# The last phase in sixteen half groups: a ring of seven PSUM banks, root arithmetic in PSUM, and TensorE filled ahead

## The reference

```python
    x = x + _layernorm(_L0_attn_ref(_layernorm(x, axis=-1), ...), axis=-1)
    x = x + _layernorm(_L0_ffn_ref(_layernorm(x, axis=-1), ...), axis=-1)

def _layernorm(x, axis=-1, eps=1e-05):
    m = jnp.mean(x, axis=axis, keepdims=True)
    v = jnp.var(x, axis=axis, keepdims=True)
    return (x - m) / jnp.sqrt(v + eps)
...
        yk = out[slot].reshape(T, K, H)
        y = jnp.sum(yk * topk_w[..., None].astype(yk.dtype), axis=1)
        shared = jax.nn.silu(x @ Sg.T) * (x @ Su.T) @ Sd.T
        return (y + shared).reshape(B, S, H)
```

## Time and profile before

| | |
|---|---|
| median of 3 runs | 1362.87 us (1362.18 to 1364.79) |
| the profiled execution | 1371.37 us |
| its span, first to last instruction | 1369.6 us |
| busy in the span | PE 89%, POOL 68%, DVE 64%, ACT 60% |
| last phase, first load's issue to the end of the span | 1307.87 to 1369.6: 61.7 us |

### The profile page before, as it was taken

One profiled execution on the slowest core, in us unless ns is written; L12 is line 12 of the kernel. 1 busy time (PEld: TensorE's weight loads), 2 busy tenths in 40 slices (PEclk: granted clock), 3 DMA queues, 4 the chain that ended last, 5 costly groups with the idle time before them and its releaser, 6 DMA issues.

```text
span 1369.6 us, 25270 instructions
## 1 busy us (share of the span) xinstructions
PE 1215.2 (89%) x7836; PEld 850.2 (62%) x7836; DVE 873.8 (64%) x2285; ACT 825.7 (60%) x2128; POOL 925.9 (68%) x1126
## 2 busy tenths in 40 slices
PE   2798989999999999999999998998866998999985
PEld 1455656666666666666666666666633677878864
DVE  5799467587679768758777875766765322232236
ACT  2566668867777776777777677777733322333313
POOL 2897556568878877986887797798754523444553
PEclk9999999999999999999999999999978999999966
DMA  7584786755555354445434444444443569898683
GB/s 229 141 221 108 179 227 154 166 108 116 122 99 117 73 111 97 83 93 101 79 79 86 97 75 85 79 72 88 78 112 118 149 183 232 234 241 197 133 252 123
DMA packets 364678, 182.68 MB, mean 133 GB/s; under 512 B 287440, under 2 KB 343222, under 8 KB 364544
## 3 DMA queue, kind: packets, MB, share of 16 engines
q1 hardware_dynamic: 344960, 166.18, 51.8%
q0 software_dynamic: 16416, 11.70, 4.8%
q10 hardware_dynamic: 3168, 3.15, 0.7%
HBM read 75.32 MB, written 64.69 MB: 102 GB/s over the span
## 4 chain that ended last, share of the span: by engine, by line
PE 38%; DVE 20%; DMA 14%; POOL 12%; issue 8%; ACT 5%; SPq 1%; another core or an unknown queue 1%; ACTq 0%; POOLq 0%; DVEq 0%
DMA PT<-PH 7%; PE bank L1035 7%; DMA Y<-W,wix 6%; PE bank L1050 6%; PE bank L1006 6%; POOL P L937 4%; POOL PH L942 4%; DVE nm L1403 4%; PE bank L1021 4%; PE bank L1067 3%; PE bank L1169 3%; PE bank L1128 2%; PE bank L1112 2%; PE bank L1182 2%; POOL BUF L697 2%
## 5 line engine op out<-in xcount | busy, mean ns | idle before, releaser
L937 POOL TENSOR_SCALAR P<-P,rr 128x256 f32<-128x256 f32 x512 | 249.2, 498 | 140.1 <-DVE rr L1399 131.7
L1265 ACT ACTIVATE P<-bank,nm 128x256 f32<-128x256 f32 x512 | 237.2, 468 | 150.5 <-DVE nm L1403 141.5
L942 POOL TENSOR_TENSOR PH<-P,PH 128x512 f16<-128x512 f32 x256 | 295.8, 1170 | 20.5 <-ACT PH L1274 19.4
L1006 PE MATMUL bank<-RB,W 128*128 128x512 f16 x1076 | 257.2, 381 | 9.0 <-ACT Sx L626 4.3
L697 POOL DMA_INDIRECT BUF<-RT,ix x192 | 198.0, 1031 | 96.5 <-issue 42.0
L1035 PE MATMUL bank<-RB 128*128 128x256 f32 x1024 | 243.9, 381 | 3.8 <-issue 2.2
L1050 PE MATMUL bank<-PT,RB 128*128 128x256 f16 x1536 | 197.7, 274 | 37.7 <-DMA PT<-PH 34.1
L1403 DVE TENSOR_REDUCE nm<-bank 128x2 f32<-128x512 f32 x256 | 174.3, 681 | 52.7 <-PE bank L1035 52.3
L1050 PEld LDWEIGHTS bank<-PT,RB 128*128 128x128 f16 x1536 | 145.8, 98 | 97.1 <-DMA PT<-PH 50.7
L1035 PEld LDWEIGHTS bank<-RB 128*128 128x128 f32 x1024 | 184.6, 190 | 26.9 <-issue 3.9
L1274 ACT ACTIVATE PH<-P 128x512 f16<-128x512 f32 x256 | 161.4, 630 | 57.6 <-POOL P L937 37.1
(11 more groups left out here) (200 smaller groups left out, 1617.7 us busy)
## 6 DMA issues: line engine op xcount, KB each, us to landing
RB<-in_ewT SPq DMA_DIRECT2D x24, 352.0 KB
BUF<-zrow SPq DMA_DIRECT2D x4, 1926.0 KB, 8.4
W<-BUF SPq DMA_DIRECT2D x64, 120.4 KB
HT<-in_ewT SPq DMA_DIRECT2D x18, 352.0 KB
HT<-in_wc SPq DMA_DIRECT2D x24, 256.0 KB, 4.7
HT<-in_ws SPq DMA_DIRECT2D x24, 256.0 KB, 5.0
Y<-zrow SPq DMA_DIRECT2D x10, 512.0 KB, 4.0
RB<-in_ewd SPq DMA_DIRECT2D x24, 176.0 KB
```

The lines of the kernel that those rows point to most:

```text
L937: r = eng.tensor_scalar(p, p, rr[:, w % 4, t:t + 1], SP_, ALU.mult, ALU.mult)
L942: eng.tensor_tensor(PH[:, w % 2, 1, :], P[:, w % 2, :], PH[:, w % 2, 0, :], ALU.subtract).then_inc(s["pl"], 1)
L1006: r = eng.matmul(bk_[:, :], W[:, m, a, c * 2048 + h * 128:c * 2048 + (h + 1) * 128], XT[:, bp % 2, b, c, :], start=(k == 0), stop=(k == n ...
L1265: r = eng.activation(P[:, u % 2, t * 256:(t + 1) * 256], bS[u % 2][:, t * 256:(t + 1) * 256], ACT.Exp, bias=nm0[:, u % 4, t:t + 1], accum_ ...
```

## The change

The unit becomes the half: index i from 0 to 15 is half i % 2 of group `GROUPS[i // 2]`, and the two late groups, 6 and 7, come first. `LB_` is a ring of seven banks with one half each. The eighth, `bP0`, holds mean, variance and the root's working values (`root`, `MV_`) and, in its upper 256 columns, a scratch product. Before the first sum TensorE writes `YL` of halves 0 to 3, then the overflow of halves 0 to 6, then eight times the same product into the scratch. From then on it takes the sum of half i and the overflow of half i + 4, which waits until half i - 3 has left its bank. The inverse root is computed as b = v*y, b = -0.5*b*y, y = (b + 1.5)*y, with v and b in PSUM and y in SBUF. Halves 13 and 15 (`MIXED`) are finished otherwise: ScalarE adds the bias to `x1`, and VectorE makes scale times bank plus that (`last_mixed`). All other residuals are POOL's. POOL's order is written anew.

```diff
-BATCH = ((0, 1), (2, 3), (4, 5), (6,), (7,))
-POOL_LAST = "s0 s1 s2 s3 x0 s4 x1 s5 x2 x3 s6 s7 x4 x5 x6 x7"
+GROUPS = (6, 7, 0, 1, 2, 3, 4, 5)
+BATCH = ((0, 1), (2, 3, 4), (5, 6, 7), (8, 9, 10), (11, 12, 13), (14, 15))
+MIXED = (13, 15)
+AHEAD = 4
+REPEATS = 8
+POOL_LAST = ("s0 s1 s2 s3 s4 s5 s6 s7 x0 s8 x1 s9 x2 s10 x3 s11 x4 s12 x5 s13 x6 s14 x7 s15 "
+             "x8 x9 x10 x11 x12 x14").split()
+DVE_LAST = "b0 b1 b2 b3 b4 b5 v13 v15".split()
...
-        LB_ = ((bACC[0], bACC[1]), (bV, bO), (bS[0], bS[1]), (bP0, bP1))
+        LB_ = (bACC[0], bACC[1], bV, bO, bS[0], bS[1], bP1)
+        NL = len(LB_)
+        root = bP0[:, 0:64].rearrange("p (k t) -> p k t", k=2)
+        MV_ = bP0[:, 128:192].rearrange("p (t n) -> p t n", n=2)
...
+            def last_part(i, part):
+                g, h = place(i)
+                if i >= NL and part != "sum" and (part == "yl" or g < LATE):
+                    if i - NL in MIXED:
+                        eng.wait_ge(s["fy"], MIXED.index(i - NL) + 1)
+                    else:
+                        eng.wait_ge(s["fn"], PLAIN.index(i - NL) + 1)
+                if part == "sum":
+                    eng.wait_ge(s["fa"], i + 1)
...
+            LATER = [i for i in range(2 * NP) if place(i)[0] >= LATE]
+            for i in LATER:
+                last_part(i, "yl")
             for k in range(4):
                 eng.wait_ge(s_o95[k], 16 * E // 4)
...
+            for i in range(NL):
+                last_part(i, "over")
+            for _ in range(REPEATS):
+                eng.matmul(bP0[:, 256:512], ident[:, :], YL[LATE][:, 0, :], start=True, stop=True)
+            for i in range(2 * NP):
+                last_part(i, "sum")
+                if NL <= i + AHEAD < 2 * NP:
+                    last_part(i + AHEAD, "over")
...
-                v, y, a, b = (fNW[:, k, c0:c1] for k in range(4))
-                step(eng.tensor_scalar(v, fMV[:, c0:c1, 1], EPS, None, ALU.add))
+                v, b = (root[:, k, c0:c1] for k in range(2))
+                y, bias = fNW[:, 1, c0:c1], fNW[:, 3, c0:c1]
+                step(eng.tensor_scalar(v, MV_[:, c0:c1, 1], EPS, None, ALU.add))
                 step(eng.tensor_scalar(y.bitcast(I32), v.bitcast(I32), -0.5, RSQRT_MAGIC, ALU.mult, ALU.add))
                 for k in range(3):
-                    step(eng.tensor_tensor(a, y, y, ALU.mult))
-                    step(eng.scalar_tensor_tensor(out=b, in0=a, scalar=-0.5, in1=v, op0=ALU.mult, op1=ALU.mult))
+                    step(eng.tensor_tensor(b, v, y, ALU.mult))
+                    step(eng.scalar_tensor_tensor(out=b, in0=b, scalar=-0.5, in1=y, op0=ALU.mult, op1=ALU.mult))
                     step(eng.scalar_tensor_tensor(out=y, in0=b, scalar=1.5, in1=y, op0=ALU.add, op1=ALU.mult))
...
+            def last_mixed(i):
+                g, h = place(i)
+                eng.wait_ge(s["fb"], MIXED.index(i) + 1)
+                for t in range(2):
+                    c, k = 2 * i + t, 2 * h + t
+                    r = eng.scalar_tensor_tensor(out=fin[g][:, 0, k, :], in0=LB_[i % NL][:, t * 256:(t + 1) * 256],
+                                                 scalar=fNW[:, 1, c:c + 1], in1=x1[g][:, k, :],
+                                                 op0=ALU.mult, op1=ALU.add)
+                r.then_inc(s["fy"], 1)
```

More of the change, by code:

```diff
@@ L29 @@
 SG, SA = 64.0, 64.0
-BATCH = ((0, 1), (2, 3), (4, 5), (6,), (7,))
-POOL_LAST = "s0 s1 s2 s3 x0 s4 x1 s5 x2 x3 s6 s7 x4 x5 x6 x7"
+GROUPS = (6, 7, 0, 1, 2, 3, 4, 5)
+BATCH = ((0, 1), (2, 3, 4), (5, 6, 7), (8, 9, 10), (11, 12, 13), (14, 15))
+MIXED = (13, 15)
+PLAIN = [i for i in range(16) if i not in MIXED]
+AHEAD = 4
[3 more added lines that the diff above has]
+DVE_LAST = "b0 b1 b2 b3 b4 b5 v13 v15".split()
 EPS = 1e-5
@@ L336, in build @@
         names = ("c0 cg cd gt S e r pn ph pl pv oh ol wo q ql k kl v vh vl xc po wm wh wl "
-                 "lf lc xr fo hd bi yi dd lb sw swh swl sg ssl saf sah sal sdn sy et ebt eg esl eac eo eow wix wt wtc fa fp fd fs fn fx fy").split()
+                 "lf lc xr fo hd bi yi dd lb sw swh swl sg ssl saf sah sal sdn sy et ebt eg esl eac eo eow wix wt wtc fa fp fd fs fn fb fx fy").split()
         s = {n: sem(f"s_{n}") for n in names + ["mx"]}
@@ L748, in build, with batch_of, place @@
         plan["sp"].setdefault(END + 101, []).append(last_rows)
-        LB_ = ((bACC[0], bACC[1]), (bV, bO), (bS[0], bS[1]), (bP0, bP1))
+        LB_ = (bACC[0], bACC[1], bV, bO, bS[0], bS[1], bP1)
+        NL = len(LB_)
+        root = bP0[:, 0:64].rearrange("p (k t) -> p k t", k=2)
+        MV_ = bP0[:, 128:192].rearrange("p (t n) -> p t n", n=2)
         def half(a, h):
             return a[:, 2 * h:2 * h + 2, :].rearrange("p t n -> p (t n)")
-        def batch_of(g):
-            return [g in b for b in BATCH].index(True)
+        def batch_of(i):
+            return [i in b for b in BATCH].index(True)
+        def place(i):
+            return GROUPS[i // 2], i % 2
         def run_plan(who, eng, slot, k=0, n=1):
@@ L893, in _ @@
                 eng.wait_ge(s_ya[k], 16 * 32)
-            for g in range(NP):
+            for g in GROUPS:
                 for k in range(2):
@@ L897, in _ @@
                         "(t p) d -> p t d", p=128)).then_inc(s_fl[g], 16)
-            for g in range(NP):
-                eng.wait_ge(s["fx"], g + 1)
-                eng.wait_ge(s["fy"], g + 1)
+            for n, g in enumerate(GROUPS):
+                eng.wait_ge(s["fx"], sum(1 for i in PLAIN if i < 2 * n + 2))
+                if any(i < 2 * n + 2 for i in MIXED):
+                    eng.wait_ge(s["fy"], sum(1 for i in MIXED if i < 2 * n + 2))
                 eng.dma_start(out[g * 512:(g + 1) * 512, :].rearrange("(t p) d -> p t d", p=128), fin[g][:, 0, :, :]
@@ L960, in _, with last_sum, last_x1 @@
                                        compute_op=ALU.add).then_inc(s_ya[e % 2], 16)
-            def last_sum(g):
+            def last_sum(i):
+                g, h = place(i)
                 f = fin[g]
                 eng.wait_ge(s_fl[g], 32)
[L965 to L971, removed]
+                eng.tensor_tensor(half(f[:, 0], h), half(f[:, 0], h), half(f[:, 1], h), ALU.add
+                                  ).then_inc(s["fa"], 1)
+            def last_x1(i):
+                g, h = place(i)
+                f = half(fin[g][:, 0], h)
+                eng.wait_ge(s["fn"], PLAIN.index(i) + 1)
                 if g < 4:
@@ L975, in last_x1 @@
                     eng.wait_ge(s["po"], PO_END)
-                eng.tensor_tensor(half(f[:, 0], 0), half(f[:, 0], 0), half(x1[g], 0), ALU.add).then_inc(s["fx"], 1)
-            for name in POOL_LAST.split():
+                eng.tensor_tensor(f, f, half(x1[g], h), ALU.add).then_inc(s["fx"], 1)
+            for name in POOL_LAST:
                 (last_sum if name[0] == "s" else last_x1)(int(name[1:]))
@@ L1196, in _ @@
             eng.wait_ge(s["wtc"], NP)
+            def last_part(i, part):
+                g, h = place(i)
+                if i >= NL and part != "sum" and (part == "yl" or g < LATE):
[6 more added lines that the diff above has]
+                for t in range(2):
+                    n = 4 * g + 2 * h + t
+                    lhs, rhs = {"yl": lambda: (ident[:, :], YL[g][:, 2 * h + t, :]),
+                                "over": lambda: (W95T[:, n * 128:(n + 1) * 128], OUT95[0:E, :]),
+                                "sum": lambda: (ident[:, :], fin[g][:, 0, 2 * h + t, :])}[part]()
+                    r = eng.matmul(LB_[i % NL][:, t * 256:(t + 1) * 256], lhs, rhs,
+                                   start=(t == 0 and (part == "yl" or part == "over" and g < LATE)),
+                                   stop=(t == 1 and part == "sum"), skip_group_check=True)
+                if part == "sum":
+                    r.then_inc(s["fp"], 1)
@@ L1354, in _ @@
                         w95_out(n)
[L1356 to L1361, removed]
+            for i in range(2 * NP):
+                g, h = place(i)
+                eng.wait_ge(s["fs"], batch_of(i) + 1)
+                if i in MIXED:
+                    if g < 4:
+                        eng.wait_ge(s["xr"], 64)
+                    else:
+                        eng.wait_ge(s["po"], PO_END)
+                for t in range(2):
+                    c, k = 2 * i + t, 2 * h + t
+                    if i in MIXED:
+                        r = eng.activation(x1[g][:, k, :], x1[g][:, k, :], ACT.Identity, bias=fNW[:, 3, c:c + 1])
+                    else:
+                        r = eng.activation(fin[g][:, 0, k, :], LB_[i % NL][:, t * 256:(t + 1) * 256],
                                            ACT.Identity, bias=fNW[:, 3, c:c + 1], scale=fNW[:, 1, c:c + 1])
-                    r.then_inc(s["fn"], 1)
+                r.then_inc(s["fb"] if i in MIXED else s["fn"], 1)
         @block.vector
@@ L1474, in step, with last_stats @@
                 eng.wait_ge(s["fd"], fd[0])
[L1476 to L1480, removed]
```

(25 more changed lines are left out.)

## The result

The changed kernel took 1376.35 us (median of 5 runs) against 1362.18 before: 1.0092 times as long, 95% interval 1.0059 to 1.0126. It is slower. The forecast was 1358.4, range 1352.3 to 1363.5.

A forecast was written before the change was run, and what follows sets the result against it. Half-clock TensorE, the batches' roots and a closing ScalarE and residual were taken to bound the last phase. Batch times summed to 1359.1 against 1363.56, a 4.5 us gain: 1362.87 - 4.5 = 1358.4, range 1352.3 to 1363.5.

The forecast's parts named there:

- The fill: TensorE before the first sum: overflow products 6.5 us and repeats 3.7 at half clock, hidden, free by 1314.2, sum at 1314.7.
- the ring: Sums wait for the batch before to be scaled: batches of three 8.6 us apart at half clock, 6.8 at full.
- The roots in PSUM: VectorE's inverse roots: 0.20 us a step, between 0.17 and 0.30, and the 1.19 us stalls beside POOL go.
- Rivals 2 and 3: Root steps in PSUM cost 0.02 to 0.10 us more, no change seen (0.20); or more still, kernel slower (0.08).
- Which clock: TensorE's clock in the last phase: half, lost in a wait after sum 5 from about 1324 to 1328.
- Rival 1: TensorE's clock stays full or comes back: last phase ends at 1353.0, 10.5 us gained, 1352.4 in all; chance 0.22.

The follow-up runs named there:

- no_repeats: The changed kernel with REPEATS 0 for 8, so no repeated scratch products: stretch 66.8 us against 63.8, ratio 1.0071 to the kernel before.
- sbuf_roots: The changed kernel with mean, variance and the root's working values back in SBUF: stretch 71.4 us against 63.8, ratio 1.0110 to the kernel before.
- zeros_in_waits: The changed kernel with 3, 6, 6 and 6 zero products behind sums 3, 5, 8 and 11: stretch 53.5 us, ratio 0.9992 to the kernel before.
- ahead2_sbuf_roots: The changed kernel with AHEAD 2 for 4 and the roots in SBUF: stretch 62.7 us, ratio 1.0086 to the kernel before.
- ahead2: The changed kernel with AHEAD 2 for 4, so the overflow of half i+2 follows sum i: stretch 44.7 us, ratio 0.9888 to the kernel before.
- ahead3: The changed kernel with AHEAD 3 for 4, so the overflow of half i+3 follows sum i: stretch 46.1 us, ratio 0.9940 to the kernel before.
- ahead2_no_repeats: The changed kernel with AHEAD 2 for 4 and REPEATS 0 for 8: stretch 45.6 us, ratio 0.9939 to the kernel before.
- mixed4_again: Second run of the changed kernel with AHEAD 2, halves 9 and 11 also taken from POOL, POOL reordered: stretch 44.7 us, ratio 0.9904 to the kernel before.

## Why the prediction was wrong, point by point

- **The fill: the time came out, its working did not.** The first sum was taken at 7.2 us into the stretch (6.8 forecast). I had written "Even at half clock TensorE is free by 1314.2". With the counts put right (see the ring, below) 14 overflow products take 11.3 us at half clock (16 took 12.9) and eight repeats 7.4, so TensorE would have been free at 1322.7, 8 us late. It came in time since the clock stayed full until 1312.3, which I had not forecast; that was luck. no_repeats puts the repeats' worth at 3.0 us.
- **The roots in PSUM: right.** Steps stand 0.20 us apart, a batch's root of six tiles takes 2.4 us, none is stalled. Rivals 2 and 3 fall, and sbuf_roots puts the gain at 7.6 us, a part of it through the clock. The 65 ns more a step that the prediction weighed from the Trainium skill, "VectorE: DVE Perf Modes", section "The TRN2 errata", did not appear: steps on 128x6 took 0.17 us here and 0.17 us in sbuf_roots.

```profile
1326.78 0.17 DVE L1517 TENSOR_SCALAR bank<-bank 128x6 f32<-128x6 f32 x1
1326.99 0.17 DVE L1518 TENSOR_SCALAR A<-bank 128x6 int32<-128x6 int32 x1
1327.19 0.17 DVE L1520 TENSOR_TENSOR bank<-bank,A 128x6 f32<-128x6 f32 x1
```

- **The ring: the mechanism was right, and its largest term was off by a factor of two. This is the step that failed.** I wrote "At half clock a pair is 0.93 us (3.71 / 4)". The earlier trace rows have x8 for one group's sums. The order lists four products for a group (two rows of x2), so the row holds two records a product, eight records are four products, and 3.71 us are two pairs. The same slip made "32 overflow products" of 16. A pair is 1.9 us by that row and 2.0 in the ring. Put right, the term is 1.09 + 4 x 2.0 + 3.79 = 12.9 us a batch, and the trace has 12.98. The sum has 14 pairs on its path (one in batch 0, two in batch 1, four each in batches 2 and 3, three in batch 4), so it grows by 15 us, from 4.5 won to 10.5 lost. The trace lost 8.1: it had the first pairs at full clock, so batch 0 was out after 13.2 us and not 13.7, and batch 1 came 7.1 us later and not 8.9. Batches 4 and 5 took 10.7 and 4.2 us, against 10.9 and 4.2. The check was at hand: in the earlier trace rows 12.9 us of half clock hold x32, and the code has 16 overflow products in all. The Trainium skill, "FP8 and Floating Point Precision", section "TensorE Precision Notes", says that true FP32 takes four passes through the array; 256 columns four times at 1.2 GHz are an estimate of 0.85 us for a product and 1.7 for a pair. The trace's 1.9 to 2.0 agrees with that far better than my 0.93.
- **Which clock: the level was right, the wait that lost it was another.** I had named a pause of some 4 us behind sum 5. The clock fell 16 us into the stretch behind a pause of 1.75 us after sum 3, where the overflow product of half 7 waits for batch 0, and stayed down for 37 us. The wait behind sum 5 measured 0.90 us.
- **Rival 1 was mis-sized by the same factor.** With the clock held, zeros_in_waits measured 53.5 us for the stretch. I had given 45.1 (1353.0 - 1307.9). At 1.06 us a pair a batch is 1.09 + 4.24 + 3.79 = 9.1 us; its trace has 9.2 between batches 2 and 3.
- **What the count hid.** With correct counts TensorE has 25 pairs after the first group has landed, 50 us at half clock. With the 7 us before the first sum that alone is more than the 55.7 us of before (an estimate, which ahead2_sbuf_roots with its 62.7 us bears out). At full clock they are 26.5 us, and POOL binds (ahead2). The worth of the change hangs on whether a pause occurs in the ring, and AHEAD 4 puts one in; even with the clock held, its order leaves 2.2 us of gain (53.5 against 55.7) where AHEAD 2 has 11.0.

What stays open: why the medians lie 10 to 14 us above those of before where the stretch gives 8.1. The intervals, 0.4 to 1.3%, allow 8.1, and for every kernel of the table the difference of its stretch to 55.7 us lies inside its interval. The 55.7 us themselves rest on one trace.

## What to carry to other kernels

Before a row of the profile is divided by its count, compare that count with the number of instructions in the code: one fp32 product stood as two records here. Where a ring of buffers refills itself in the instruction stream of the engine that also does the urgent work, count how far behind the released buffer stands: two halves less of lead took no work away and was worth 19 us. And on TensorE a short pause is not priced by its length: a 1.75 us wait brought 37 us at half clock, and padding the waits with products of zeros gave 10 us back.

## What the runs showed of the hardware

- Pauses of 0.66 us between pairs left the granted clock at 1.00 (ahead3), where the same ring with a pause of 1.75 us, or 3.12 us in ahead2_sbuf_roots, lost it. In these two the fall came 2.0 and 1.5 us after work had been taken up again; in a pause of 5.36 us (no_repeats) it came in the pause, after 3.8 us.
- Alternating pairs of 64 and 128 rows, 28 us without a gap at 0.50, did not raise the clock (ahead2_sbuf_roots), while the same pairs at 1.00 with gaps of 0.25 us kept it (ahead2). Products of 128 rows alone had it back in 6.0 us in ahead2_no_repeats, 4.4 us in mixed4_again and 4.5 us at the end of the changed kernel. Whether the 64 rows are the reason no run tells.
- A VectorE step on 4 to 6 columns takes 0.16 to 0.17 us with tiles in PSUM, written and read, as with tiles in SBUF. With all tiles in SBUF single steps took 1.13 to 1.19 us beside GpSimd's additions (sbuf_roots, ahead2_sbuf_roots); in the changed kernel none did.
- Products with zeros held the clock as others do: 1.00 from 1328 to 1346 in zeros_in_waits.
